# Values and sums of the exponentials of a windowed attention in four column tiles, with the own heads picked by DMA

## The chip, the cores and the metric

The kernel runs on one core of a Trainium2 chip. The metric is the device time of one execution in microseconds. A core has the engines PE (TensorE, matrix products), DVE (VectorE), ACT (ScalarE, activations), POOL (GpSimd) and SP (SyncE, which here only issues DMAs). Each runs its own instruction stream in order, and they meet at semaphores.

## The reference

Two layers over 8 sequences of 512 tokens with 128 channels. Layer 0 adds to x a Mamba block (projection, convolution, a scan with 16 states over time, gate) and a mixture of eight experts. Layer 1 is the part that the change touches:

```python
xn = layernorm(x)
q, k, v = split_heads(xn @ Wq + bq), split_heads(xn @ Wk + bk), split_heads(xn @ Wv + bv)   # 16 heads of 8
probs = softmax(q @ k.T / sqrt(8) + mask)        # mask: |i - j| <= 32
x = x + (probs @ v) @ Wo + bo + (silu(xn @ wg) * (xn @ wu)) @ wd
```

## The kernel before

**The order of the work.** Every engine walks through the same list of units. One turn of the list is an iteration of 28 slots. Three lanes run in it, each for another sequence: `pre` (projections and convolution for the next sequence), `scan` (the scan of layer 0: 16 steps, in slots 0, 1, 3, 5, 7, 8, 10, 12, 14, 15, 17, 19, 21, 22, 24, 26) and `attn` (layer 1 of the sequence before). `finish` is the end of layer 1 of the sequence before that one. The tables PRE_AT, LAYER1_AT, FINISH_AT and EDGE say in which slot a unit stands; EDGE's come first in slot 0, and within a slot the order is exp, values, scores, step, averages, sum, rowmax, turn, then finish, attn and pre. Eight sequences give seven iterations with both a scan and attention, one with attention alone, and a last one with only the finish.

**A step of the scan** is on VectorE the scan (L705, 128x1024) and the product dBu (L697), on ScalarE two exponentials dA (L901), on GpSimd the product hc (L1066), and on TensorE the sum into y_bank (L1151). At the end of the scan y_bank is gated (L800), and TensorE multiplies with out_proj (L1196).

**Attention.** 512 queries are 16 groups g of 32. The 128 partitions hold 4 heads x 32 queries, and r = 0 to 3 counts four such sets (a head is 8 of the 32 channels of a set r). For each group: `scores` (L1224, L1226) writes 128 x 4 x 96 into a PSUM bank, `rowmax` (DVE L820), `exp` (ACT L983, four instructions), `turn` (four transposes L1232 to PSUM, and ACT's copy pT, L988). Every second group there is a unit of `values` (L1240): with pT as the stationary operand it gives 128 partitions (head, query) x 33 columns, the 32 channels of all four heads of a set and, since vw has a column of ones, the sum of the exponentials; the 33 columns are computed three times (VREP) and read once. `averages` on VectorE takes the reciprocal of the sums (L831) and multiplies, in four instructions, each head's own 8 channels by it (L835). In slot 0 of the next iteration `attnT` transposes the averages (L1252, L1254), ACT adds the bias bv (L994); in slot 3 `fin` (L1261, L1266, L1270) adds the feed-forward part and the product with Wo, and in slot 4 `y_out` (DVE L848) adds x1.

**Banks.** Layer 1 has three PSUM banks, called work, work_l and more in the profile (0, 1, 2 in L1_BANK), which its units take in a fixed turn: `fin` uses 0, as do out, q, v1, the even scores and turns; the values and the gates of the feed-forward part use 2.

**Tables of ScalarE.** Functions come in table sets. The loads stand where the function changes: ahead of the logarithm (L944, slot 24) and ahead of the next exponential.

**SP's queue** issues the rows of B and C for each step of the scan (L526, three steps ahead), x_in, x_res and the output. The chip's time before the first attention iteration (some 245 us) goes to the experts and the first scan.

## Time and profile before

| | |
|---|---|
| median of 3 runs | 1190.73 us (1190.7 to 1194.21) |
| profiled execution, its own time | 1193.12 us |
| its span, first to last instruction | 1191.1 us |
| mean granted TensorE clock | 0.923 of full speed |
| busy: PE, DVE, ACT, POOL | 78%, 71%, 51%, 35% of the span |

The rows in the section on the trace come from this one profiled execution. Busy shares are means over the whole span. In a row, "x16" is the number of instructions merged into it; "[0.76 <-ACT pT L988]" says how long the engine had been idle and which instruction released it. A float32 matrix product is two instructions in the trace (two passes), a transpose one. A term of a sum is compared with the profiled execution's 1193.12 us, and a forecast with the median.

### The profile page before, as it was taken

The numbers are of one execution on the slowest core, as the hardware profiler recorded it, in microseconds if no ns is written. First come the engines' busy times: TensorE is split into PE (matmuls) and PEld (weight loads), VectorE is DVE, ScalarE is ACT, GpSimd is POOL, SyncE is SP. The second block draws the span as 40 slices with busy tenths as digits, with TensorE's granted clock in tenths as the row PEclk, the third lists the DMA queues.
The fourth block names the chain that finished last, engine by engine and source line by source line (L and its number), as shares of the span: only waits on it lengthen the run. The fifth ranks groups of instructions, "written<-read, shape, count | busy, mean of one in ns | idle before, by whom it ended". The sixth has DMA issues, their size and how long they took to land.

```text
span 1191.1 us, 13478 instructions
## 1 busy us (share of the span) xinstructions
PE 923.4 (78%) x4474; PEld 585.3 (49%) x4474; DVE 849.0 (71%) x1301; ACT 613.0 (51%) x1410; POOL 411.1 (35%) x234
## 2 busy tenths in 40 slices
PE   3553888857887788778887788878787878788786
PEld 2412676734554455545454455545554545445555
DVE  7772543669779877888688868886978788767232
ACT  2142555635655655564566455655645564654542
POOL 2274222233622362237213722363226423532000
PEclk9566999987999899999999899989998999999998
DMA  8163878843322332233223321333233223430000
GB/s 277 40 216 125 235 234 294 239 110 86 81 65 75 90 82 73 66 79 89 73 70 90 89 73 54 90 92 87 54 80 87 76 66 83 99 80 1 10 1 9
DMA packets 79540, 116.65 MB, mean 98 GB/s; under 512 B 4848, under 2 KB 40048, under 8 KB 79344
## 3 DMA queue, kind: packets, MB, share of 16 engines
q1 hardware_dynamic: 73184, 108.99, 33.5%
q0 software_dynamic: 6288, 6.82, 2.5%
q8 instruction: 35, 0.57, 0.2%
q14 instruction: 33, 0.27, 0.1%
HBM read 103.73 MB, written 12.06 MB: 97 GB/s over the span
## 4 chain that ended last, share of the span: by engine, by line
PE 37%; DVE 19%; issue 17%; POOL 13%; ACT 10%; DMA 3%; SPq 0%; POOLq 0%; DVEq 0%; ACTq 0%
PE y_bank L1151 11%; DVE hst L705 7%; POOL hc L1066 7%; PE more L1240 7%; POOL xs_d L1034 3%; POOL x_res L1050 3%; ACT pexp L983 3%; PE work_l L1232 3%; DVE dBu L697 2%; ACT pT L988 2%; PE work_l L1226 2%; PE work L1232 2%; PE work L1170 2%; DMA hst<-in_hidden 1%; PE more L1248 1%
## 5 line engine op out<-in xcount | busy, mean ns | idle before, releaser
L1066 POOL TENSOR_TENSOR hc<-hst,bcr 128x1024 f32<-128x1024 f32 x116 | 280.2, 2415 | 607.8 <-DVE dBu L697 607.8
L1151 PE MATMUL y_bank<-hc,pk 128*128 128x512 f32 x512 | 275.0, 664 | 68.6 <-POOL hc L1066 59.7
L705 DVE TENSOR_TENSOR_SCAN hst<-dA,dBu 128x1024 f32<-128x1024 f32 x128 | 291.6, 2278 | 5.7 <-ACT dA L901 4.9
L1151 PEld LDWEIGHTS y_bank<-hc,pk 128*128 128x128 f32 x512 | 100.6, 208 | 183.9 <-POOL hc L1066 83.9
L901 ACT ACTIVATE dA<-dt,neg_a 128x511 f32<-128x511 f32 x256 | 171.4, 726 | 17.3 <-DVE hst L705 15.8
L697 DVE TENSOR_TENSOR dBu<-dtu,bcr 128x1024 f32<-128x1024 f32 x128 | 157.9, 1234 | 12.7
L1240 PE MATMUL more<-vw,pT 96*128 96x99 f32 x1024 | 131.0, 280 | 37.3 <-ACT pT L988 25.9
L1240 PEld LDWEIGHTS more<-vw,pT 96*128 96x128 f32 x1024 | 121.2, 194 | 69.3 <-issue 38.1
L988 ACT COPY pT<-work 96x512 f32<-96x512 f32 x64 | 37.2, 581 | 157.4 <-PE work L1232 157.4
L820 DVE TENSOR_REDUCE nmax<-work 128x4 f32<-128x384 f32 x64 | 35.4, 554 | 62.6 <-PE work L1226 62.6
L988 ACT COPY pT<-work_l 96x512 f32<-96x512 f32 x64 | 37.2, 581 | 63.9 <-PE work_l L1232 63.9
L983 ACT ACTIVATE pexp<-work,nmax 128x96 f32<-128x96 f32 x256 | 65.8, 343 | 6.3 <-DVE nmax L820 6.1
L983 ACT ACTIVATE pexp<-work_l,nmax 128x96 f32<-128x96 f32 x256 | 65.9, 341 | 5.7 <-DVE nmax L820 5.5
L835 DVE TENSOR_TENSOR attn<-more,rden 32x64 f32<-32x64 f32 x256 | 55.9, 218 | 8.1
L1050 POOL DMA_INDIRECT x_res<-ys_d,slot_b x32 | 51.8, 1620 | 9.3 <-issue 9.3
L1232 PEld LDWEIGHTS work_l<-pk,pexp 128*96 128x96 f32 x256 | 28.0, 127 | 51.0 <-ACT pexp L983 31.2
L1226 PE MATMUL work_l<-kT,qbd 128*128 128x384 f32 x128 | 52.3, 490 | 0.0
L1226 PE MATMUL work<-kT,qbd 128*128 128x384 f32 x128 | 51.8, 487 | 0.0
L1232 PEld LDWEIGHTS work<-pk,pexp 128*96 128x96 f32 x256 | 29.9, 127 | 41.2 <-issue 20.7
L1164 PE MATMUL work<-xnT,pk 128*128 128x512 f32 x64 | 38.4, 686 | 14.2 <-ACT hs L914 9.4
L1232 PE MATMUL work_l<-pk,pexp 128*96 128x128 f32 x256 | 39.7, 277 | 12.4 <-ACT pexp L983 12.1
L1232 PE MATMUL work<-pk,pexp 128*96 128x128 f32 x256 | 40.2, 281 | 11.8 <-ACT pexp L983 11.8
(296 smaller groups left out, 1422.0 us busy)
## 6 DMA issues: line engine op xcount, KB each, us to landing
bcr<-bc_d SPq DMA_DIRECT2D x128, 512.0 KB, 4.9
qbd<-in_wx SPq DMA_DIRECT2D x8, 578.0 KB, 3.9
attn<-in_wx SPq DMA_DIRECT2D x8, 578.0 KB, 4.3
pT<-in_wx SPq DMA_DIRECT2D x8, 578.0 KB, 5.7
kT<-in_wx SPq DMA_DIRECT2D x8, 578.0 KB, 5.3
vw<-in_wx SPq DMA_DIRECT2D x8, 578.0 KB, 5.0
xs_d<-rbuf POOLq DMA_DIRECT2D x1, 2560.0 KB, 9.7
hst<-in_hidden SPq DMA_DIRECT2D x8, 256.0 KB, 5.8
```

The lines of the kernel that those rows point to most:

```text
L697: v.tensor_tensor(dBu[:], dtu[par], bcr[n % RING][:, 0:1, :].to_broadcast([P, NH, L]), ALU.mult).then_inc(s_dBu, 1)
L705: v.tensor_tensor_scan(hst[n % 2][:].rearrange("p h t -> p (h t)"), dA[n % 2][:].rearrange("p h t -> p (h t)"), dBu[:].rearrange("p h t -> ...
L835: last = v.tensor_tensor(attn[:, k - 1:k + 1, :, j, :], o[q, :, :, HD * j:HD * j + HD], rden[q, :, :].unsqueeze(3).to_broadcast([32, 2, RG ...
L901: s.activation(dA[n % 2][:, h, 1:L], dt[par][:, h, 1:L], ACT.Exp, scale=neg_a[:, h, n:n + 1]).then_inc(s_dA, 1)
L983: last = s.activation(pexp[k % 2][:, r, :], w1k(f"s{k}")[:, r * KW:(r + 1) * KW], ACT.Exp, bias=nmax[:, k, r:r + 1])
L988: s.copy(pT[k % 4][:], w1k(f"pT{k}")[0:KW, :]).then_inc(free1(f"pT{k}"), 1)
L1050: g_.indirect_dma_start(x_res[:, j, :], None, ys_d.rearrange("i j p d -> (i j p) d"), bass.IndirectOffsetOnAxis(ap=slot_b[:, j:j + 1], axi ...
L1066: g_.tensor_tensor(hc[n % 2][:], hst[n % 2][:], bcr[n % RING][:, 1:2, :].to_broadcast([P, NH, L]), ALU.mult).then_inc(s_hc, 1)
L1151: last = t.matmul(y_bank[h][:], ident, hc[n % 2][:, h, :], start=False, stop=(n == N - 1))
L1226: t.matmul(w1k(key)[:, 0:RG * KW], qbd[:, k, :, :].rearrange("p h q -> p (h q)"), kT[:, :, k * GQ:k * GQ + KW], start=False, stop=True).th ...
L1232: last = t.transpose(w1k(key)[0:KW, r * P:(r + 1) * P], pexp[k % 2][:, r, :], ident)
L1240: last = t.matmul(w1k(key)[:, a:a + VREP * 33].rearrange("p (n d) -> p n d", n=VREP), pT[(k - 1 + c) % 4][:, r * P:(r + 1) * P], vw[:, k - ...
```

## The change

What was the averages on VectorE becomes a chain over four engines. The roles in `values` are swapped: vw is now stationary (96 x 32 channels of a set r), pT is moving (128 columns: 4 heads x 32 queries), and the result of set r goes to the partitions 32r to 32r + 31. A second matmul with 32 columns of ones as the stationary operand gives the sums of the exponentials on the same partitions. ScalarE copies both to o_all in SBUF. Of the four heads in the columns each partition needs its own, so SP issues 16 DMAs for each half of a sequence, one for each block of 8 partitions, from o_all to o_own. VectorE takes one reciprocal for each half, GpSimd multiplies the whole sequence, ScalarE adds bv. TensorE's transposes fall away. The finish moves: own1 in slot 0, rec1 and avg in slot 5, attnT in slot 6, fin in slot 7, y_out in slot 8. After the last tanh of the feed-forward part the table set with both logarithm and exponential is loaded.

```diff
-VREP = 3
+OWN = 16 * 16
-LAYER1_AT = {0: ["out"], 1: ["x1"], 2: ["ln_a"], 3: ["ln_b"], 4: ["q", "k"], 5: ["v0", "v1"], 6: ["v2", "v3"]}
-FINISH_AT = {2: ["attnT"], 3: ["fin"], 4: ["y_out"]}
-EDGE = [("attn", "y_end"), ("finish", "attnT"), ("pre", "xnT"), ("attn", "gated"), ("attn", "out")]
+LAYER1_AT = {0: ["out"], 1: ["x1"], 2: ["ln_a"], 3: ["ln_b"], 4: ["q", "k"], 5: ["v0", "v1"], 6: ["v2", "v3"], 19: ["own0"], 21: ["rec0"]}
+FINISH_AT = {0: ["own1"], 5: ["rec1", "avg"], 6: ["attnT"], 7: ["fin"], 8: ["y_out"]}
+EDGE = [("attn", "y_end"), ("finish", "own1"), ("pre", "xnT"), ("attn", "gated"), ("attn", "out")]
...
-        vw_all = sb("vw", [P, G, RG, HD * 4 + 1])
+        vw_all = sb("vw", [P, G, RG, HD * 4])
-        attn_all = sb("attn", [P, G, RG, 4, HD])
+        o_all = sb("o_all", [P, 4, 2, G // 2, GQ])
+        ones_v = sb("ones_v", [P, 32])
+        o_own = rbuf[:]
...  SP
+                    if name in ("own0", "own1"):
+                        k = int(name[3:])
+                        q = slice(k * L // 2, (k + 1) * L // 2)
+                        done1(sp, b, f"o{4 * k + 3}")
+                        before(sp, s_avg, b)
+                        for r in range(RG):
+                            for h in range(4):
+                                own = slice(32 * r + HD * h, 32 * r + HD * h + HD)
+                                sp.dma_start(o_own[own, :, q], o_all[own, h, :, :, :].rearrange(
+                                    "p c g q -> p c (g q)")).then_inc(s_own, 16)
...  VectorE
-                    v.memset(vw, 1.0).then_inc(s_clear, 1)
+                    v.memset(ones_v[:], 1.0).then_inc(s_clear, 1)
+                elif name in ("rec0", "rec1"):
+                    k = int(name[3:])
+                    q = slice(k * L // 2, (k + 1) * L // 2)
+                    dve.wait_ge(s_own, (2 * b + k + 1) * OWN)
+                    v.reciprocal(o_own[:, 1, q], o_own[:, 1, q]).then_inc(s_rden, 1)
-                elif name == "averages":
-                    ...
-                    v.reciprocal(rden[:], o[:, :, :, 32]).then_inc(s_rden, 1)
-                    dve.wait_ge(s_rden, b * (G // 2) + k // 2 + 1)
-                    for j in range(4):
-                        last = v.tensor_tensor(attn[:, k - 1:k + 1, :, j, :], ...)
...  ScalarE
                 elif name == "ffn":
                     s.activation(fth[:], w1k(f"gate{k}")[:], ACT.Tanh).then_inc(s_fth, 1)
+                    if k == HC - 1:
+                        s.preload_act_table_set("natural_log_exp_and_others")
+                elif name == "averages":
+                    key = f"o{k // 2}"
+                    full1(act, b, key)
+                    if k in (1, 9):
+                        before(act, s_own, (2 * b + k // 8) * OWN)
+                    g = (k - 1) % 8
+                    for j in range(2):
+                        last = s.copy(o_all[:, :, j, g:g + 2, :].rearrange("p h g q -> p g h q"),
+                                      w1k(key)[:, 2 * P * j:2 * P * j + 2 * P].rearrange("p (g h q) -> p g h q", g=2, h=4))
+                    last.then_inc(free1(key), 1)
                 elif name == "attnT":
-                    full1(act, b, name)
-                    s.activation(attnT[:], w1k(name)[:], ACT.Identity, bias=pc("bv")).then_inc(free1(name), 1)
+                    act.wait_ge(s_avg, b + 1)
+                    done1(act, b, f"up{HC - 1}")
+                    s.activation(attnT[:], fth[:], ACT.Identity, bias=pc("bv")).then_inc(s_attnT, 1)
...  GpSimd
+                    elif name == "avg":
+                        pool.wait_ge(s_rden, 2 * b + 2)
+                        done1(pool, b, f"gate{HC - 1}")
+                        g_.tensor_tensor(fth[:], o_own[:, 0, :], o_own[:, 1, :], ALU.mult).then_inc(s_avg, 1)
...  TensorE
                         for r in range(RG):
-                            a = (c * RG + r) * 33
-                            last = t.matmul(w1k(key)[:, a:a + VREP * 33].rearrange("p (n d) -> p n d", n=VREP),
-                                            pT[(k - 1 + c) % 4][:, r * P:(r + 1) * P],
-                                            vw[:, k - 1 + c, r, :].unsqueeze(1).to_broadcast([KW, VREP, 33]),
-                                            start=True, stop=True)
+                            t.matmul(w1k(key)[32 * r:32 * r + 32, c * P:(c + 1) * P], vw[:, k - 1 + c, r, :],
+                                     pT[(k - 1 + c) % 4][:, r * P:(r + 1) * P], start=True, stop=True)
+                        for r in range(RG):
+                            last = t.matmul(w1k(key)[32 * r:32 * r + 32, (2 + c) * P:(3 + c) * P], ones_v[0:KW, :],
+                                            pT[(k - 1 + c) % 4][:, r * P:(r + 1) * P], start=True, stop=True)
-                elif name == "attnT":
-                    ...
-                    for g in range(G):
-                        last = t.transpose(w1k(name)[:, g * GQ:(g + 1) * GQ],
-                                           attn[:, g, :, :, :].rearrange("p r h d -> p (r h d)"), ident[0:GQ, 0:GQ])
```

## Rows read from the trace of the kernel before

**Rows 1.** The page's part 1: busy us, share of the span, instructions
```profile
PE 923.4 (78%) x4474; PEld 585.3 (49%) x4474; DVE 849.0 (71%) x1301; ACT 613.0 (51%) x1410; POOL 411.1 (35%) x234
```

**Rows 2.** Busy us of each engine in slots 5-9, 15-20 and 21-27
```profile
643.50:664.20 20.70, 14.53 (x65) 8.89 (x64) 20.28 (x16) 12.63 (x21) 7.48 (x3) 0.84 0.39 94
682.50:711.90 29.40, 25.82 (x119) 14.83 (x119) 19.16 (x31) 16.55 (x45) 8.70 (x4) 1.00 0.30 80
711.90:743.90 32.00, 26.45 (x135) 17.01 (x136) 28.57 (x41) 18.15 (x39) 7.04 (x3) 0.95 0.17 50
```

**Rows 3.** Line L800: ns min/median/max, first and last start
```profile
L800 DVE TENSOR_TENSOR dtu<-y_bank,sg x16: 680/686/692, 244.7 to 1100.4; 128x512 f32<-128x512 f32 x16
```

**Rows 4.** The chain that ended last: start, us, what
```profile
605.51 0.45 PE work_l L1232 x4
...
616.59 2.01 PE more L1240 x16
```

**Rows 5.** Groups of instructions: out<-in xcount | busy us, mean ns | idle
```profile
L1066 POOL TENSOR_TENSOR hc<-hst,bcr 128x1024 f32<-128x1024 f32 x116 | 280.2, 2415 | 607.8 <-DVE dBu L697 607.8
...
L835 DVE TENSOR_TENSOR attn<-more,rden 32x64 f32<-32x64 f32 x256 | 55.9, 218 | 8.1
...
L988 ACT COPY pT<-work 96x512 f32<-96x512 f32 x64 | 37.2, 581 | 157.4 <-PE work L1232 157.4
...
L831 DVE RECIPROCAL rden<-more 128x8 f32<-128x8 f32 x64 | 13.1, 204 | 47.8 <-PE more L1240 47.4
...
L884 ACT ACTIVATE pT<-work 128x128 f32<-128x128 f32 x14 | 3.9, 276 | 25.5 <-PE work L1122 25.5
...
L755 DVE TENSOR_REDUCE ss<-xsq 128x4 f32<-128x256 f32 x8 | 3.3, 412 | 1.4 <-ACT xsq L928 1.4
...
L679 DVE MEMSET vw<- 96x2112 f32 x1 | 1.8, 1818 | 0.4 <-issue 0.4
```

**Rows 6.** Timeline of slots 21-27: start, us, engine, line [idle <-releaser]
```profile
716.92 0.58 ACT L988 COPY pT<-work 96x512 f32<-96x512 f32 x1 [3.66 <-PE work L1232]
...
726.56 1.88 PE L1151 MATMUL y_bank<-hc,pk 128*128 128x512 f32 x4
...
729.52 1.28 ACT L944 ACT_TABLE_LOAD   x1
...
734.27 0.95 PE L1232 MATMUL work<-pk,pexp 128*96 128x128 f32 x4 [1.82 <-ACT pexp L983]
...
735.02 3.30 PE L1151 MATMUL y_bank<-hc,pk 128*128 128x512 f32 x4
...
739.51 2.00 PE L1240 MATMUL more<-vw,pT 96*128 96x99 f32 x16 [0.76 <-ACT pT L988]
...
742.79 1.23 DVE L697 TENSOR_TENSOR dBu<-dtu,bcr 128x1024 f32<-128x1024 f32 x1
```

**Rows 7.** The timeline of slots 3 and 4
```profile
641.04 0.69 DVE L848 TENSOR_TENSOR y_out<-x1r,work 128x512 f32<-128x512 f32 x1 [5.39 <-PE work L1270]
...
642.27 0.60 ACT L919 ACTIVATE tg<-work 128x512 f32<-128x512 f32 x1 [0.28 <-PE work L1164]
```

**Rows 8.** The timeline of slots 8 and 9
```profile
658.54 3.78 PE L1151 MATMUL y_bank<-hc,pk 128*128 128x512 f32 x4 [5.02 <-POOL hc L1066]
...
662.11 2.24 PE L1170 MATMUL work<-pk,u 128*128 128x96 f32 x16
```

**Rows 9.** The timeline of the iteration with attention alone
```profile
1119.70 0.53 PE L1224 MATMUL work<-bandb,identb 128*128 128x384 bf16 x1
```

**Rows 10.** SP's queue: a DMA issue of 64 KB
```profile
688.66 0.32 SPq L533 DMA_DIRECT2D bc_d<-dtT  x1
```

**Rows 11.** DMA issues: out<-in xcount, KB each, median us to landing
```profile
bcr<-bc_d SPq DMA_DIRECT2D x128, 512.0 KB, 4.9
...
bc_d<-dtT SPq DMA_DIRECT2D x8, 64.0 KB, 1.7
```

**Rows 12.** The timeline of the tail; the span ends at 1191.1
```profile
1187.67 0.69 DVE L848 TENSOR_TENSOR y_out<-x1r,work 128x512 f32<-128x512 f32 x1 [7.34 <-PE work L1270]
```

32 lines of the change are left out of this document (9 added, 23 removed).

## The prediction, made before the changed kernel had run

> **What bounds the kernel now.** The page comes first, for the balance of the engines: TensorE is busy for 78% of the span and VectorE for 71% [rows 1], so neither average decides; they are both full somewhere, and the question is where. The table of stretches splits one steady iteration (L800, which opens one, runs in pairs from 244.7 to 1100.4 us, so seven iterations with a scan take 122.2 us each; one with attention alone follows, and a tail) [rows 2, 3]. What the reader should see: in slots 5 to 9 (643.5 to 664.2) VectorE is busy 20.3 of 20.7 us; in slots 15 to 20 (682.5 to 711.9) TensorE is busy 25.8 of 29.4; in slots 21 to 27 both are nearly full, VectorE 28.6 and TensorE 26.5 of 32.0. So the same microsecond is worth something different in each stretch, and I make the sum by stretch.
>
> **The values and their row sums.** Now a unit is 8 matmuls with the 96x128 pT stationary and 99 columns moving; the trace has two passes for each, and the chain shows 16 passes in 2.01 us, 0.125 each [rows 4]. After: 16 matmuls, 32 passes, 32 stationary columns and 128 moving ones. The trace has a pass with 128 moving columns and 96 stationary ones, the transposes of L1232: four in 0.45 us, 0.112 each [rows 4]. Their smaller stationary operand did not hold them back, so I take 0.112 as the time for which a pass streams. One after another, 32 passes would be 3.6 us, 1.6 more than now. No two matmuls of this trace write different groups of 32 partitions, so whether column tiles run side by side is not shown. Bounds: 3.6 us, and a quarter of it, 0.9, if four always ran together. I take a value between: the two passes of one matmul need the same tile and can't overlap, and they are issued back to back; so if matmuls begin in order, the second pass of one tile can run only beside the first pass of the next. That makes 17 streams of 0.112, 1.9 us, a gain of 0.1. The nearest rows speak for order: in every group of matmuls the passes stand in the order in which they were issued.
>
> The Trainium skill (TensorE: Matmul & The Clock Gate, section Part 3: Packing small matmuls) says that column tiles run concurrently and that matmuls start and end strictly in order; it gives 2.38x for three column tiles with 512 columns. By that speedup alone a unit would be 3.6 / 2.38 = 1.5 us (an estimate); by its rule of order it is my 1.9. The page on TensorEngine Tiling (Array Packing), section Key Properties, adds that a change of the mode drains the array, which this kernel would pay twice in a unit. No run here shows any of the three yet.
>
> **What leaves VectorE, and what comes.** Each unit loses one reciprocal of 0.20 us and four products of 0.22: 1.1 us in 64 units [rows 5]. ScalarE gets two copies of 256 columns: between the 0.28 us of 128 columns and the 0.58 us of 512 lies 0.38, so 0.75 us a unit [rows 5]. They stand ahead of the copy of pT in ScalarE's queue, and that copy waits for TensorE, 3.66 us before 716.92 [rows 6], so they are hidden; without that cover they would cost 0.75 x 64 = 48 us. Two reciprocals of 128x256 per sequence are new. The trace has only 128x8 at 204 ns. The products of 64 columns take 218 ns and a reduction of 256 takes 412, 1.0 ns a column and 153 to start; so the 8 columns cost 51 ns, some 6 ns each [rows 5]. Bounds for 256 columns: 0.42 us if those 51 ns are a fixed cost, 1.7 us at 6 ns a column. I take 1.7, as the one row of this operation has it. (The Trainium skill, VectorE: DVE Perf Modes, section First, the fixed hardware budget, says that a reciprocal runs with a repeat count of 8. At its 0.96 GHz that would be 2.1 us and the start, an estimate on the same side.)
>
> **Slots 21 to 27.** VectorE loses three units there (3.5 us and a wait of 1.2) and gains the first reciprocal, 1.7. The table load of 1.28 us ahead of the logarithm goes, and the second one behind it, ahead of the exponentials [rows 6]: with them TensorE waited 1.82 us for the exponentials and then ran four passes of L1151 in 3.30 us, which take 1.88 at the full clock. The load moves behind the last tanh in slot 20, ahead of the same wait of 3.66 us [rows 6]. I follow the two queues from 711.9. The first reciprocal makes step 13 begin 0.7 us late; the missing averages give this back by step 14; the transposes of group 14 start at 732.5 instead of 734.3; values 15 start at 736.8 instead of 739.5 [rows 6]. VectorE is then the later one: steps 15, hc, dtu and dBu end at 741.3 instead of 744.0, because 1.2 of averages and 1.0 of waiting drop out in front of dBu. The gated product follows at once: **-2.7 us** an iteration. The transposes of attnT on TensorE in slot 0 lie in the shadow of the gated product: nothing.
>
> **Slots 0 to 9.** Here lies the largest wait that the change removes: VectorE stands 5.39 us before y_out, because fin is in front of it, and conv1 is queued behind [rows 7]. But what is late next? sg0, behind conv1, wants tanh of zg0 (642.27 [rows 7]), and that follows ScalarE's normalised rows and a TensorE transpose, not fin. It gains about 1.6 us, and pays 1.28 for the table load that now stands before this tanh: -0.4. From there VectorE is full to slot 9, and gets the second reciprocal (+1.7) and y_out (+0.7). Sum: **+2.0**. Fin (32 passes and the one of the bias, some 4 us on TensorE by the pass of [rows 4]) fills the hole of 5.02 us before 658.54, which also spares the passes behind it the low clock (3.78 us instead of 1.88 [rows 6, 8]). X_dbl, now at 662.11, could then follow u, which VectorE has ready at 660.8; y_out makes u 0.7 late, and the rest of that wait goes: **-0.6**. GpSimd's product is half of the 2.42 us of 128x1024, 1.2 us, and lies in the 608 us in which it waits for VectorE [rows 5].
>
> **Slots 10 to 20.** TensorE is the bound (VectorE is busy 19.2 of 29.4 us [rows 2]); averages that stand ahead of a row maximum cost only where the exponentials wait for it, for which I give half of one unit's 1.1: -0.5. Five units give 5 x 0.1: **-1.0** together.
>
> An iteration is -2.7 + 2.0 - 0.6 - 1.0 = -2.3, seven of them -16.1.
>
> **The ends.** In the iteration with attention alone TensorE has no hole in slot 7: the first scores start at 1119.70 right behind v3 [rows 9]. Fin (4.0 at the full clock, 0.5 more for a cold start) and y_out (0.7) now lie between, since both use one bank: +5.2; the units give 0.8 back: **+4.4**. At the very end the chain is now: values end 1179.1, two copies 0.75, sixteen DMA issues, the landing, reciprocal 1.7, product 1.2, attnT 0.69, eight passes of wo at half the clock 8 x 2 x 0.112 = 1.8, y_out 0.69, and 2.7 from there to the end [rows 12]. The issue of 64 KB takes 0.32 us of SP, and they land in 1.7 us [rows 10, 11]: 16 x 0.34 = 5.4 and 1.7. That ends at 1195.9 instead of 1191.1: **+4.8**. The memset of vw, 1.82 us, becomes one of 32 columns [rows 5]: **-1.7**.
>
> Sum: -16.1 + 4.4 + 4.8 - 1.7 = -8.6 us against the profiled execution's 1193.1, which stands 2.4 above the median of 1190.7 (its span is 1191.1, so 2.0 lie around it). On the scale of the median: 1182.
>
> **SP's queue.** In slots 15 to 20 three units take 29.4 us [rows 2], 9.8 each. The sixteen issues in slot 19 begin with the copies of unit 7, take 5.4 us and land 1.7 later, 7.1 in all; ScalarE's copy of unit 9, which waits for them, is ready 9.8 after that of unit 7: 2.7 us of slack. The rows of B and C for step 14 are issued behind them and land 4.9 us later [rows 11], 10.7 after the copies of unit 7; the product that wants them follows step 13 in slot 22, some 16 after them. In slot 0 the rows of step 3 stand behind the issues in the same way, and have two steps and a slot without a step to spare; x_in stands there too, which nobody wants before the next iteration.
>
> **The rivals.**
> 1. *Tiles exclude each other* (slower). A unit takes 3.6 us, 1.7 above my value. It costs 43 units in full (five of each full iteration, all eight of the last), 73 us, and the other 21 some 21 after VectorE's slack: 1182 + 94 = 1276. For it: the trace shows no overlap of any two passes. Against: separate groups of columns. It decides from 2.1 us a unit on.
> 2. *All four tiles overlap.* A unit of 0.9 to 1.4 us, since 32 weight loads have a price that no row shows alone: 43 x 0.5 to 1.0 = 22 to 43 us less, some 1150. Against it stand the two passes of each matmul. (The page's 1.5 us for a unit would give 1182 - 43 x 0.4 = 1165, an estimate.)
> 3. *The reciprocal costs as little as another operation*, 0.42 us: 1.3 x 15 = 19 us less, 1163.
> 4. *The picks come late.* At 0.6 us an issue the sixteen take 9.6 and 1.7, and unit 9 waits 1.5 us, and the rows of B and C behind them as much: 10 to 25 us more, 1192 to 1207. It decides from 0.5 us an issue on.
>
> **Chances.** Forecast 0.40 (its own range 1170 to 1197), serial tiles 0.18, four-fold overlap 0.15, cheap reciprocal 0.13, late picks 0.14. The predicted time is 1182. A range from 1140 to 1235 leaves out the serial tiles and little else. Within 0.3% (3.6 us, about what this kernel's measurements tell from nothing) lies a quarter of the forecast and a little of the fourth rival: 0.13. Faster: 0.52, of which 0.24 from the forecast and 0.28 from the second and third rivals. Slower: 0.35.
>
> **What would show it.** The unit's length on TensorE in the iteration without a scan (1.9; 3.6 or 1.2 for the rivals); the mean of the new reciprocal (1.7); no wait of ScalarE before the unit 9 copies for a DMA; one table load in slot 20 and one before the tanh of zg0; no 5.4 us wait before y_out, but VectorE full from slot 4 on; scores 5 us later after v3 in the last iteration; a tail 5 us longer. The prediction is wrong if a unit is not near 1.9 us, since each 0.1 us there is 4 us of time, or if TensorE's clock, which is at its lower level behind the hole before 658.54 [rows 8], falls in slots 3 and 4 too, where fin leaves a hole.

## The result: 1197.99 us, slower by 0.4%

| | median us (runs) | ratio to before, 95% interval |
|---|---|---|
| before | 1193.89 (1190.7 to 1196.67, 20 runs) | |
| after | 1197.99 (1193.43 to 1207.09, 20 runs) | 1.0039 (1.0026 to 1.0052) |

The forecast was 1182 and faster. The time lies in the range and on the other side of no change. The twenty executions of after spread over 14 us, and the time goes with the granted clock (0.919 in the shortest, 0.901 in the longest). The profiled execution of after took 1201.56 us, its span is 1199.5, and its mean granted clock 0.915. The page shows less work on TensorE and VectorE [rows 1] and a longer span:

```profile
PE 874.3 (73%) x5362; PEld 510.9 (43%) x5362; DVE 828.6 (69%) x997; ACT 649.5 (54%) x1541; POOL 422.7 (35%) x242
```

The two halves of the span go in opposite directions. The gated product, one for each iteration (L812 in after, L800 before), is the mark: its first pair starts at 242.6 us (244.7 before), its last at 1091.6 (1099.8 before). So the seven iterations between take 849.0 us, 6.1 less than before. The first and the last of the seven are shorter by 4.0 us each; the five between take 615.0 us together, and 613.0 before. But from the last gated product to the end it is 107.9 us, and 91.3 before: 16.6 more. With the 2.1 us of the start that is 8.4, the whole difference of the spans. Forecast were -16.1, +9.2 and -1.7.

### What the trace of after shows

Groups of instructions by line and form (busy us, mean ns of one, idle time before them):

```profile
L709 DVE TENSOR_TENSOR dBu<-dtu,bcr 128x1024 f32<-128x1024 f32 x128 | 167.6, 1309 | 16.0 <-DMA bcr<-bc_d 3.1 <-DVE hst L717 0.5
...
L744 DVE SCALAR_TENSOR_TENSOR z<-hs,half_c,z 128x512 f32<-128x512 f32 x48 | 56.3, 1223 | 0.0
...
L1002 ACT COPY o_all<-more 128x256 f32<-128x256 f32 x128 | 41.7, 385 | 60.2 <-DMA rbuf<-o_all 35.5 <-PE more L1260 24.7
...
L834 DVE RECIPROCAL rbuf<-rbuf 128x256 f32<-128x256 f32 x16 | 28.0, 1750 | 44.5 <-DMA rbuf<-o_all 44.5
...
L795 DVE TENSOR_TENSOR dc<-tg,dc 128x1024 f32<-128x1024 f32 x8 | 14.4, 1794 | 0.5 <-ACT tg L945 0.5
...
L1100 POOL TENSOR_TENSOR fth<-rbuf 128x512 f32<-128x512 f32 x8 | 12.4, 1549 | 91.8 <-DVE rbuf L834 91.8
```

The reciprocal of 256 columns takes 1.75 us (forecast 1.7), the copy 0.385 (0.38). New is the waiting: ScalarE stands 35.5 us in all before its copies for the picks' DMA, and VectorE 44.5 us before the reciprocals. And VectorE's operations on other lines have become slower: L744 1223 ns in place of 1049, L795 1794 in place of 1224, dBu 1309 in place of 1234.

The line of the picks in SP's queue (ns min/median/max, first and last start):

```profile
L554 SPq DMA_DIRECT2D rbuf<-o_all x256: 679/686/1292, 331.7 to 1187.9; - x128
```

The timeline of one iteration (its gated product is at 617.0 us): the passes behind fin in slot 8 (653.38), the collision in slots 12 to 14 (671.76), the picks of slot 19 and who waits for them, the last passes and the next gated product (736.53); then a unit of values without a scan beside it (1124.89), and the tail:

```profile
653.38 3.15 PE L1169 MATMUL y_bank<-hc,pk 128*128 128x512 f32 x4 [2.93 <-POOL hc L1080]
...
671.76 2.93 POOL L1080 TENSOR_TENSOR hc<-hst,bcr 128x1024 f32<-128x1024 f32 x1
...
673.59 3.01 DVE L709 TENSOR_TENSOR dBu<-dtu,bcr 128x1024 f32<-128x1024 f32 x1
674.08 1.43 POOL L1073 TENSOR_TENSOR xdn<-xdr,pk 128x384 f32<-128x384 f32 x1
...
674.74 3.56 PE L1169 MATMUL y_bank<-hc,pk 128*128 128x512 f32 x4 [1.96 <-POOL hc L1080]
...
699.61 11.65 SPq L554 DMA_DIRECT2D rbuf<-o_all  x16
...
712.64 1.75 DVE L834 RECIPROCAL rbuf<-rbuf 128x256 f32<-128x256 f32 x1 [1.99 <-DMA rbuf<-o_all]
712.70 0.65 ACT L1002 COPY o_all<-more 128x256 f32<-128x256 f32 x2 [3.98 <-DMA rbuf<-o_all]
...
713.88 0.50 PE L1242 MATMUL work<-bandb,identb 128*128 128x384 bf16 x1 [3.80 <-ACT pT L989]
...
715.45 3.61 PE L1169 MATMUL y_bank<-hc,pk 128*128 128x512 f32 x4
...
736.53 3.39 PE L1169 MATMUL y_bank<-hc,pk 128*128 128x512 f32 x4 [1.53 <-DVE hc L732]
...
739.96 1.29 DVE L812 TENSOR_TENSOR dtu<-y_bank,sg 128x512 f32<-128x512 f32 x2 [1.08 <-PE y_bank L1169]
...
1124.89 0.43 PE L1257 MATMUL more<-pT,vw 96*32 96x128 f32 x8 [1.50 <-DVE fsg L841]
...
1125.13 0.40 PE L1260 MATMUL more<-pT,ones_v 96*32 96x128 f32 x8
...
1125.35 0.40 PE L1257 MATMUL more<-pT,vw 96*32 96x128 f32 x8
...
1125.57 0.40 PE L1260 MATMUL more<-pT,ones_v 96*32 96x128 f32 x8
...
1125.90 0.34 PE L1242 MATMUL work_l<-bandb,identb 128*128 128x384 bf16 x1
...
1175.99 0.65 ACT L1002 COPY o_all<-more 128x256 f32<-128x256 f32 x2 [1.28 <-PE more L1260]
...
1176.66 11.96 SPq L554 DMA_DIRECT2D rbuf<-o_all  x16
1190.02 1.75 DVE L834 RECIPROCAL rbuf<-rbuf 128x256 f32<-128x256 f32 x1 [18.01 <-DMA rbuf<-o_all]
1191.85 1.26 POOL L1100 TENSOR_TENSOR fth<-rbuf 128x512 f32<-128x512 f32 x1 [85.35 <-DVE rbuf L834]
```

How to read it. The four groups of eight passes start 0.22 us apart, and the next matmul of another kind follows 1.01 us after the first (1124.89 to 1125.90): a unit is 1.0 us, not 1.9, and not 2.01 as before [rows 4]. The sixteen picks in slot 19 hold SP for 11.65 us, 0.73 each, where the prediction had 5.4 in all. ScalarE's copy of unit 9 starts at 712.70, 3.98 us late; pT is queued behind it, so TensorE stands 3.80 us, and the passes behind the hole run at the lower of its two levels, 1.2 GHz in place of 2.4 (L1169: 3.61 us in place of 1.88 [rows 6]; granted clock 0.53 in these 3.6 us). VectorE's first reciprocal waits 1.99 us for the same picks. In the tail the picks hold SP for 11.96 us, and the reciprocal starts 13.4 us after the first issue.

Count also the groups of four passes into y_bank that run wholly or in part at the lower level. Before there are three in an iteration: in slot 1, in slot 8 and in slot 26 [rows 6, 8]. In this iteration of after there are four: behind a hole of 2.93 us in slot 8, behind 1.96 us at 674.74, behind the picks, and behind 1.53 us at 736.53. For the last of them the next gated product waits 1.08 us. So fin has not filled the hole in slot 8, it has shortened it from 5.02 to 2.93 us, and the passes behind it still take 3.15 us.

The starts of the groups' scores (L1242; L1224 before) in us after the gated product, worked out from the timelines of one iteration each:

```
group             0     4     5    11    12    13    next gated product
before          43.1  57.0  63.3  92.6  96.4 102.5   122.9
after           41.7  54.9  63.6  90.0  96.9 104.3   123.0
```

This is the table that says where the gain went. Up to group 4 after is 2.1 us ahead. From 4 to 5 it loses 2.4. From 5 to 11 it gains 2.9, three units of one microsecond each. From 11 to 13 it loses 4.4 to the picks. The rest is 1.7 shorter. Sum: 0.1. The means of the five middle iterations say the same (group 4 at 54.9 for 56.7, group 5 at 63.9 for 63.0, group 11 at 90.6 for 92.3, group 13 at 104.4 for 102.2, the gated product at 123.0 for 122.6).

### The profile page after: what moved, and what is told of

It reads as the page before. It is cut to its first block, busy times and chain, and to the rows that moved or that the text cites. A ratio compares the mean times of both kernels' runs of the same rounds, so it can differ in the third digit from the quotient of the medians.

```text
span 1199.5 us, 15327 instructions
## 1 busy us (share of the span) xinstructions
PE 874.3 (73%) x5362; PEld 510.9 (43%) x5362; DVE 828.6 (69%) x997; ACT 649.5 (54%) x1541; POOL 422.7 (35%) x242
## 4 chain that ended last, share of the span: by engine, by line
PE 29%; DVE 24%; issue 15%; ACT 11%; POOL 10%; SPq 7%; DMA 4%; DVEq 0%; POOLq 0%; ACTq 0%
PE y_bank L1169 9%; DVE hst L717 8%; SPq L554 7%; POOL x_res L1064 4%; POOL hc L1080 3%; POOL xs_d L1048 3%; DVE dBu L709 3%; DVE z L744 2%; ACT pT L989 2%; PE work_l L1250 2%; ACT pexp L984 2%; ACT dA L902 2%; PE work L1244 1%; DMA hst<-in_hidden 1%; PE more L1257 1%
## 5 line engine op out<-in xcount | busy, mean ns | idle before, releaser
L1169 PE MATMUL y_bank<-hc,pk 128*128 128x512 f32 x512 | 279.9, 674 | 74.6 <-POOL hc L1080 57.1
L1169 PEld LDWEIGHTS y_bank<-hc,pk 128*128 128x128 f32 x512 | 102.6, 211 | 189.9 <-issue 91.6
L709 DVE TENSOR_TENSOR dBu<-dtu,bcr 128x1024 f32<-128x1024 f32 x128 | 167.6, 1309 | 16.0 <-DMA bcr<-bc_d 3.1
L1257 PE MATMUL more<-pT,vw 96*32 96x128 f32 x1024 | 54.9, 282 | 39.3 <-ACT pT L989 25.9
L837 DVE TENSOR_REDUCE nmax<-work_l 128x4 f32<-128x384 f32 x64 | 35.5, 554 | 59.0 <-PE work_l L1244 58.9
L1002 ACT COPY o_all<-more 128x256 f32<-128x256 f32 x128 | 41.7, 385 | 60.2 <-DMA rbuf<-o_all 35.5
L1242 PE MATMUL work<-bandb,identb 128*128 128x384 bf16 x64 | 22.3, 348 | 61.2 <-ACT pT L989 60.2
L834 DVE RECIPROCAL rbuf<-rbuf 128x256 f32<-128x256 f32 x16 | 28.0, 1750 | 44.5 <-DMA rbuf<-o_all 44.5
L1257 PEld LDWEIGHTS more<-pT,vw 96*32 96x32 f32 x1024 | 27.7, 110 | 71.7 <-issue 38.4
L744 DVE SCALAR_TENSOR_TENSOR z<-hs,half_c,z 128x512 f32<-128x512 f32 x48 | 56.3, 1223 | 0.0
L1260 PE MATMUL more<-pT,ones_v 96*32 96x128 f32 x1024 | 54.3, 277 | 0.0
```

The costliest lines, as they stand in the source:

```text
L709: v.tensor_tensor(dBu[:], dtu[par], bcr[n % RING][:, 0:1, :].to_broadcast([P, NH, L]), ALU.mult).then_inc(s_dBu, 1)
L744: v.scalar_tensor_tensor(z[k % 2][:, h, :], hs[:, h, tap:tap + L], half_c[:, h * KC + tap:h * KC + tap + 1], z[(k - 1) % 2][:, h, :], ALU. ...
L1169: last = t.matmul(y_bank[h][:], ident, hc[n % 2][:, h, :], start=False, stop=(n == N - 1))
L1257: t.matmul(w1k(key)[32 * r:32 * r + 32, c * P:(c + 1) * P], vw[:, k - 1 + c, r, :], pT[(k - 1 + c) % 4][:, r * P:(r + 1) * P], start=True, ...
```

## The experiments

Each kernel is timed against the kernel before on the same chip; the ratio is to that. Those of the picks, the tiles and the last queue start from after, those whose name begins with "before" or "finish" from before.

### Do column tiles run side by side?

**One tile**, and **pairs on a tile**:

```diff
 one_tile
-  t.matmul(w1k(key)[32 * r:32 * r + 32, c * P:(c + 1) * P], vw[...], pT[...])     # ones alike
+  t.matmul(w1k(key)[0:32, c * P:(c + 1) * P], vw[...], pT[...])
 pairs_on_a_tile
-  for r in range(RG): values(c, r)
-  for r in range(RG): ones(c, r)
+  for r in range(RG): values(c, r); ones(c, r)
```

> The changed kernel with all sixteen matmuls of a values unit writing partitions 0 to 31, that is, one column tile in place of four; the results of three of the four row groups are not written. The order of two and two on one tile cost nothing to speak of (a unit 1.06 us in place of 1.01). Theory 'column tiles run side by side, and the chip looks past the two matmuls ahead of it': with one tile nothing can run side by side, 32 passes of 0.11 us, 3.5 us a unit, and 40 to 60 such units: 1300 to 1350 us. Rival 'a pass with a stationary operand of 32 columns is simply short (0.027 us), whichever tile it is in': a unit stays at 1.0, and the time at 1198 within 5 us.

> The changed kernel with the same sixteen matmuls of a values unit in another order: values and ones of one column tile behind one another, so that four passes in a row want the same tile. In the changed kernel eight passes of four tiles take 0.22 us, as though all four tiles ran side by side. Theory 'tiles run side by side, and matmuls begin in order': 25 streams of 0.11 us are left in a unit, 2.8 us in place of 0.9; with 40 to 60 units that count, 1275 to 1310 us. Rival 'the passes are short for another reason' or 'each tile has its own queue, whatever the order': no change, 1198 within 3 us.

One tile (three quarters of the results are not written): 1294.11 us, 1.0837 (1.0823 to 1.0851). Pairs on a tile: 1203.32, 1.0087 (1.0068 to 1.0107). The values in the iteration with attention alone, first one tile, then pairs (here ones is L1259):

```profile
1221.88 1.03 PE L1257 MATMUL more<-pT,vw 96*32 96x128 f32 x8 [0.76 <-ACT pT L989]
...
1222.75 1.04 PE L1260 MATMUL more<-pT,ones_v 96*32 96x128 f32 x8
...
1223.63 1.04 PE L1257 MATMUL more<-pT,vw 96*32 96x128 f32 x8
...
1224.50 1.04 PE L1260 MATMUL more<-pT,ones_v 96*32 96x128 f32 x8
```

```profile
1128.21 0.45 PE L1257 MATMUL more<-pT,vw 96*32 96x128 f32 x8 [1.50 <-DVE fsg L841]
...
1128.45 0.43 PE L1259 MATMUL more<-pT,ones_v 96*32 96x128 f32 x8
...
1128.67 0.44 PE L1257 MATMUL more<-pT,vw 96*32 96x128 f32 x8
...
1128.89 0.44 PE L1259 MATMUL more<-pT,ones_v 96*32 96x128 f32 x8
...
1129.27 0.34 PE L1242 MATMUL work_l<-bandb,identb 128*128 128x384 bf16 x1
```

In one tile eight passes take 0.875 us, 0.109 each, which is the pass of the prediction; in four tiles 0.22. So the four tiles run fully side by side. A unit is 2.5 us longer in one tile, 160 us in 64 units, of which 96 show in the time. A unit in four tiles takes 1.01 us where its 32 passes, four abreast, make 0.87: the change to column tiles and back costs no more than the rest. Pairs on one tile, four passes in a row for the same tile, take 1.06 us a unit in place of 1.01: the chip isn't held up by the order of issue over that distance, which the prediction's 17 streams suppose. What it does inside isn't shown, only that this order costs 0.05 us a unit.

The Trainium skill (TensorE: Matmul & The Clock Gate, section Part 3: Packing small matmuls) has column tiles running concurrently, and the trace agrees: four tiles give 0.875 / 0.22, about 4.0, where the skill's page has 2.38 for three, with 512 columns. By its words that matmuls start and end strictly in order, and if passes on one tile wait for each other, pairs on a tile should have held up the rest; the runs don't bear out the two together, and which of them fails isn't shown.

### What do the picks cost?

```diff
 two_buffers
-  o_all = sb("o_all", [P, 4, 2, G // 2, GQ])
+  o_all = sb("o_all", [P, 2, 4, 2, G // 2, GQ])          # one for each half
 one_pick
-  for r in range(RG):
-      for h in range(4): sp.dma_start(o_own[own, :, q], o_all[own, h, :, :, :])
+  sp.dma_start(o_own[:, :, q], o_all[:, 0, :, :, :])
 picks_in_one_piece
-  sp.dma_start(o_own[own, :, q], ...)                    # two pieces of 1 KB a partition
+  sp.dma_start(o_own[own, k, :], ...)                    # one of 2 KB
```

> The changed kernel with a second copy of o_all, so that ScalarE's copies of unit 9 need not wait for the picks of the first half; the picks themselves stay. Theory 'late picks': in the changed kernel ScalarE waits 4.0 us for the picks in slot 19 (35.5 us in the eight waits together), TensorE stands 3.8 us behind it and then runs at its lower clock. With the wait gone an iteration gets 4 to 6 us shorter, 8 of them 32 to 48: 1150 to 1166 us. Rival 'VectorE decides behind it': the wait lies in front of slots 21 to 27, where VectorE is the bound, so that it only moves: 1188 to 1198, and VectorE is then busy without a gap in slots 21 to 27.

> The changed kernel with one DMA for each half in place of sixteen: it takes the columns of head 0 of each group for all 128 partitions, so the values of the other heads are not the right ones; bytes and everything else are the same. Theory 'late picks': no wait of ScalarE in slot 19, rows of B and C not behind sixteen issues, and a tail 11 us shorter (0.4 in place of 11.6): 8 x 4 to 6 and 11, 1139 to 1155 us. Rival 'VectorE decides': the tail's 11 and no more, 1187. It also prices the sixteen issues against the second copy: the difference to that run is the tail's 11 and what the rows of B and C wait.

> The changed kernel with the picked rows laid out by half, so that each pick writes 2 KB in one piece for each partition and not two of 1 KB. If the 0.68 us of SP for an issue goes with the number of pieces, it falls to some 0.35 us, sixteen take 5.5 us, and the time falls to 1150 to 1170 (with 'late picks'). If it is the price of any small DMA here, it stays 0.68 us, and the time 1198 within 3 us.

| kernel | us | ratio (95%) |
|---|---|---|
| two_buffers | 1199.3 | 1.0059 (1.0039 to 1.0078) |
| one_pick | 1156.75 | 0.97 (0.9675 to 0.9725) |
| picks_in_one_piece | 1185.71 | 0.9941 (0.9929 to 0.9954) |

One pick in place of sixteen (it brings the values of head 0 to all) gives some 41 us against after; of these 20 lie behind the last gated product (87.4 us to the end, 107.9 in after). The sixteen issues are the cost. But a second buffer, which removes ScalarE's wait entirely, gives nothing: in one iteration group 12 comes at 93.3 and group 13 at 99.4 in place of 96.9 and 104.3, and then VectorE waits for the same picks before the first reciprocal, and group 14 is 5.5 us behind group 13 (2.1 in before):

```profile
711.86 1.75 DVE L834 RECIPROCAL rbuf<-rbuf 128x256 f32<-128x256 f32 x1 [1.98 <-DMA rbuf<-o_all]
```

The issue of a pick (the source line of each kernel, ns min/median/max):

```profile
L551 SPq DMA_DIRECT2D rbuf<-o_all x16: 599/600/666, 334.9 to 1144.7; - x16
```

```profile
L554 SPq DMA_DIRECT2D rbuf<-o_all x256: 624/625/1440, 334.4 to 1178.8; - x128
```

The pick of 128 partitions costs SP 600 ns, the one of 8 partitions in two pieces 686, in one piece 625. Neither partitions nor pieces make it dear. Reading SBUF doesn't either: in after the output (out from y_out, L558) reads it and takes 0.38 us, and bc_d from dtT, the row that the prediction used, takes 0.32 [rows 10]; both write DRAM. A bcr issue (L528) reads DRAM and writes SBUF, 0.36. What the picks have and none of these has is SBUF at both ends; no other DMA of that kind was tried. The 61 ns a pick are 1 us for each sixteen, and the time falls by more than 10 us. The expectation had 0.35 us an issue, or no change; it was neither.

Then both deadlines at once, and each alone:

```diff
 one_late_rec (second buffer, one piece), late_rec_one_buffer (one buffer)
-  19: ["own0"], 21: ["rec0"]
+  19: ["own0"]
-  5: ["rec1", "avg"]
+  5: ["rec", "avg"]                                      # v.reciprocal of 2 x 256 columns
```

> The changed kernel with the second copy of o_all, the picked rows in one piece, and one reciprocal of 512 columns in slot 5 in place of one in slot 21 and one in slot 5. With the second copy alone the time stayed at 1199: ScalarE's wait was gone, but VectorE waited 2.0 us for the same picks ahead of the first reciprocal. Theory 'two deadlines on one set of picks': with both gone, the picks cost nothing in slots 19 to 21, and an iteration is as short as with one pick (118.7 us in place of 122.9): 7 x 3 to 4 us less than 1186 of the picks in one piece, 1158 to 1168. Rival 'slots 4 to 9 are full on VectorE': moving 1.7 us of reciprocal there costs as much as it gives, 1180 to 1190.

> The kernel with one late reciprocal, but with the single o_all of the changed kernel: the fourth corner of a square. Picks in one piece in all: both deadlines 1185.7 (measured), neither 1171.5 (measured); the second copy alone took nothing off the changed kernel. Theory 'either deadline alone holds slots 19 to 21': ScalarE still waits 3.4 us in slot 19, the scores of group 12 stay 3 us late, and most of this reaches the gated product: 1180 to 1186. Rival 'only VectorE's deadline counts, because slots 21 to 27 are VectorE's': 1171 to 1174.

| in one piece | reciprocal in slot 21 and 5 | one in slot 5 |
|---|---|---|
| one buffer | 1185.71, 0.9941 | 1189.01, 0.9976 (0.9965 to 0.9987) |
| two buffers | not run (in two pieces: 1199.3) | 1171.5, 0.9821 (0.9795 to 0.9847) |

Neither deadline alone gives time, with one piece a pick the moved reciprocal even costs 3; with both gone 14 us come off at once. Where they come off, in the profiled executions (us):

| | first and last of the seven iterations | the five between | behind the last gated product |
|---|---|---|---|
| picks_in_one_piece (both deadlines) | 235.0 | 603.9 | 106.2 |
| late_rec_one_buffer (ScalarE's) | 233.6 | 600.9 | 108.7 |
| one_late_rec (none) | 228.4 | 596.7 | 99.9 |
| one_pick | 228.3 | 594.5 | 87.4 |

Behind the last gated product either deadline alone is enough to hold the work: of the 17 us between the second and the third row 8.8 lie there, and two_buffers, which has VectorE's deadline alone, needs 107.2 there. In the five middle iterations this isn't shown. With the reciprocal moved and one buffer ScalarE still waits 3.0 us, but four of the five take 119.3 to 119.6 us, as long as with both deadlines gone (118.3 to 120.5), and one takes 123.2. The measured 1189 is above what either theory gave for this kernel (1180 to 1186, 1171 to 1174). An experiment that takes away one of two waits for the same event shows nothing, and that isn't evidence against the event.

```diff
 last_on_two_queues: of the second half's sixteen picks in the last two sequences, eight issued by ScalarE
 tail_by_halves: in the last sequence reciprocal and product of the first half before the last picks land
 spread_picks: four picks a slot, in slots 19 to 22 and 0 to 3; each of the three stands on the one before, the first on one_late_rec
-  19: ["own0"]
+  19: ["own00"], 20: ["own01"], 21: ["own02"], 22: ["own03"]
```

> The kernel with one late reciprocal, and the second half's picks of the last two sequences issued by SP and ScalarE, eight each, in place of sixteen by SP. Behind the last values nothing but the picks is left, and behind the sequence before them fin waits in front of the scores. Theory: the tail is 8 x 0.62 = 5 us shorter and the start of the last sequence's scores up to 4 us earlier: 7 to 9 us less than the kernel with one late reciprocal. Rival 'the two queues share what makes an issue slow': 1.2 us for an issue, and no change.

> The kernel with the last picks on two queues, and in the last sequence the reciprocal and GpSimd's product taken for each half by itself, so that the first half's are out of the way before the last picks land. The tail loses 1.7 us of reciprocal and 0.6 of product: 2.3 us less than the kernel with the last picks on two queues, 1163 to 1167. A rival only in size: GpSimd's second product beside nothing, so that no more than the reciprocal's 1.7 comes off.

> The kernel with the tail by halves, and the sixteen picks of a half in four slots, four each, in place of one run of ten us in SP's queue. In the kernel with one late reciprocal VectorE waits 16.4 us in all for rows of B and C that are issued behind the picks (3.1 us in the changed kernel, where other waits covered it). Theory: that wait goes, and 8 to 16 us with it: 1150 to 1158. Rival 'the wait lies in slack': nothing, 1163 to 1167.

1167.83, 0.9781 (0.9768 to 0.9793); 1164.97, 0.9778 (0.9765 to 0.979); 1160.81, 0.9734 (0.9713 to 0.9755). Eight issues on each of two queues take 5.6 and 6.0 us side by side, so the queues don't share what makes an issue slow. The first gives some 4 us of the 7 to 9 expected. The step from the first to the second is within the intervals; their traces have 95.7 and 93.6 us behind the last gated product (99.9 in one_late_rec), near the 2.3 expected. In the third VectorE's wait for rows of B and C, 16.6 us in all, is gone, as the theory has it, and 4 us of the 8 to 16 come off.

### The other parts alone, and why they don't add up

```diff
 before_finish
-FINISH_AT = {2: ["attnT"], 3: ["fin"], 4: ["y_out"]}
+FINISH_AT = {6: ["attnT"], 7: ["fin"], 8: ["y_out"]}
 before_table
+                    if k == HC - 1: s.preload_act_table_set("natural_log_exp_and_others")
 before_finish_table: both; finish_table_late_bc and spread_late_bc: bc (xdn) in slot 14, not 13
```

> The kernel before with one part of the change alone: the transposes of attnT in slot 6, fin in slot 7, y_out in slot 8 (before: 2, 3, 4). By the prediction's steps, without table and reciprocal: sg0 1.6 us earlier, y_out 0.7 in the full stretch, 0.6 from the hole, so 1.5 us less in each of seven iterations, and 5.2 more in the iteration with attention alone: 1192 - 10 + 5 = 1187. Rival 'VectorE loses it to GpSimd': the convolution's products, which now start 5 us earlier, lie beside GpSimd's product of 128x1024 and get slower (3.51 us for two in place of 1.4 in the changed kernel): 1193 to 1200.

> The kernel before with one part of the change alone: the table of the logarithm and the exponential loaded behind the last tanh, in slot 20. The prediction has 1.28 us for the load ahead of the logarithm and as much for the second behind it, both in front of the exponentials for which TensorE waited 1.82 us and ran 1.4 us at its lower clock. If that is worth what the prediction gave: 1.0 to 2.5 us in each of eight iterations, 8 to 20 us, 1171 to 1183. Rival 'ScalarE is ahead of VectorE there': no change, 1190 to 1193.

> The kernel before with the finish in slots 6 to 8 and the table loaded in slot 20, the values as they were. Alone the two gave 13.0 and 4.3 us. If they add up: 1174. Then the values in tiles with well-placed picks (1160.8) are worth 13 us, most of it in the iteration with attention alone. Rival 'TensorE has no slack in slots 21 to 27, so the table needs the shorter units': 1177 to 1180. Rival 'the values in tiles are worth nothing': 1158 to 1163.

> The kernel before with finish, table and GpSimd's product xdn in slot 14. If the side by side of dBu and GpSimd costs here as well (the scores of group 5 start 7.6 us after those of group 4 with the finish moved, 6.3 in the kernel before): 1 to 2 us an iteration, 1160 to 1167. If it is only the slot that changes: 1172 to 1176.

| kernel | us | ratio (95%) |
|---|---|---|
| before_finish | 1178.4 | 0.9894 (0.9878 to 0.9909) |
| before_table | 1189.38 | 0.9963 (0.995 to 0.9976) |
| before_finish_table | 1189.66 | 0.9987 (0.9973 to 1.0001) |
| finish_table_late_bc | 1189.67 | 0.9986 (0.9966 to 1.0006) |

The moved finish is by itself worth 13 us, twice its forecast, and it loses nearly all of it when the table moves too. Putting xdn one slot later in that kernel changes nothing (1189.67). The traces say part of why the gain is lost. The timelines of three kernels, at the passes into y_bank that follow a hole (slot 1 and slot 8 of before; the same two of before_finish; slot 14 of two iterations of before_finish_table):

```profile
751.35 3.65 PE L1151 MATMUL y_bank<-hc,pk 128*128 128x512 f32 x4 [2.12 <-POOL hc L1066]
...
781.47 3.78 PE L1151 MATMUL y_bank<-hc,pk 128*128 128x512 f32 x4 [5.02 <-POOL hc L1066]
```

```profile
743.14 1.98 PE L1151 MATMUL y_bank<-hc,pk 128*128 128x512 f32 x4 [2.12 <-POOL hc L1066]
...
769.99 1.98 PE L1151 MATMUL y_bank<-hc,pk 128*128 128x512 f32 x4 [1.15 <-POOL hc L1066]
```

```profile
796.72 1.99 PE L1153 MATMUL y_bank<-hc,pk 128*128 128x512 f32 x4 [1.62 <-POOL hc L1068]
...
916.87 3.43 PE L1153 MATMUL y_bank<-hc,pk 128*128 128x512 f32 x4 [1.63 <-POOL hc L1068]
```

Read the number in brackets and then the duration. The same 2.12 us of idle time is followed by 3.65 us for four passes in before and by 1.98 in before_finish, where the hole of 5.02 us in slot 8, which fin now fills, has become 1.15. That the one brings the other isn't shown: in before itself the hole of 2.12 us is once followed by four passes in 1.98 us (at 384.12, in the second iteration). In the steady iteration of before_finish the granted clock is 1.00 throughout, in before it is 0.94, with three slow groups an iteration; the iteration takes 119.1 us for 122.9. And in before_finish_table a hole of 1.62 us leaves the clock alone in one iteration, and one of 1.63 in the next brings 3.43 us: iterations of 120.1 and 121.9 us take turns. So the time here depends on whether the clock falls behind a hole, and this on more than the hole's length. It isn't all: without a slow group this iteration still takes 120.1 us for 119.1, and of the 11.8 us between the two spans 3.9 lie behind the last gated product. For these no cause was looked for.

The last two runs put work into the holes and move nothing:

```diff
 before_filled {0: 10, 4: 26}, spread_filled {0: 10, 4: 20, 7: 10, 14: 6}
+                for _ in range({0: 10, 4: 26}.get(n, 0)):
+                    t.matmul(y_bank[0][:, 0:RG * KW], nil[:], bandb[:, 1, :, :].rearrange("p r k -> p (r k)"),
+                             start=False, stop=False)
                 pe.wait_ge(s_hc, b * N + n + 1)
```

> The kernel before, unchanged but for 10 and 26 such matmuls in front of the sums of steps 0 and 4 (holes of 2.1 and 5.0 us). If the clock alone makes the 3.8 us that the finish gives in an iteration (119.1 in place of 122.9), filling the holes gives as much without moving anything: 2 x 1.7 us an iteration, 1192 - 8 x 2 to 3.5: 1164 to 1176. If the gain of the moved finish was VectorE's wait before y_out, which stays here: 1190 to 1195.

> The kernel with spread picks, and in front of the sums of steps 0, 4, 7 and 14 (where TensorE stands 2.1, 3.8, 2.3 and up to 1.5 us) 10, 20, 10 and 6 matmuls of 128x384 bf16 with a stationary operand of zeros, which add nothing to y_bank; the queue runs them before the wait. Theory 'the clock is what the shorter units give back': the passes behind the holes, 3.4 to 3.8 us in slots 1, 8 or 26, take 1.98, two such groups an iteration are gone, 3.2 us, of which half to all shows: 1135 to 1150. Rival 'the fill is in the way, or zeros do not keep the clock': 1158 to 1175.

1181.62, 0.9906 (0.9881 to 0.9931), and 1157.82, 0.9707 (0.9695 to 0.972), 35 us under the kernel before; only one_pick, which picks one head for all, is as fast. before_filled at the places of before's 751.35 and 781.47:

```profile
746.42 1.79 PE L1152 MATMUL y_bank<-bandb,nil 128*128 128x384 bf16 x10
...
748.04 1.88 PE L1156 MATMUL y_bank<-hc,pk 128*128 128x512 f32 x4
...
771.18 4.39 PE L1152 MATMUL y_bank<-bandb,nil 128*128 128x384 bf16 x26
...
776.37 1.98 PE L1156 MATMUL y_bank<-hc,pk 128*128 128x512 f32 x4 [0.80 <-POOL hc L1068]
```

Matmuls that add zeros stand where TensorE stood idle (L1152), and the four passes behind them take 1.88 and 1.98 us. Nothing else has changed but the passes' own time, so the gain of 11 us is the clock's; the mean granted clock of the execution is 0.962 in place of 0.923, and 1.00 in a steady iteration. It is less than the 16 to 28 us expected. A steady iteration takes 120.1 us, 2.8 less than before, and before_finish has 3.8 less: the clock is worth most of what the moved finish gives, and the rest may be the wait before y_out or what the fill itself costs. In the spread kernel the same fill takes nearly all slow groups away too (0.955 for 0.930), and gives only 3 us where 11 to 26 were expected; what holds the iteration there instead was not tried.

### What is left of the units' gain?

> The kernel with spread picks, with a reciprocal of 8 columns in place of 512 in all sequences but the last, so that the averages of these are not divided rightly. Theory 'slots 4 to 9 are VectorE's': 3.1 us of 3.35 go, and nearly all of it shows: 7 x 3.1 = 22 us, 1139 to 1145. Rival 'it lies under the exchange of TensorE and ScalarE': 1155 to 1161.

> The kernel with spread picks, and GpSimd's product xdn in slot 14 in place of 13. In the kernel with one late reciprocal that product and the one of hc lie beside VectorE's dBu of step 7, which takes 3.15 us where it takes 1.23 alone, and the scores of group 5 start 7.4 us after those of group 4 (6.3 in the kernel before). Theory 'side by side they slow each other': dBu falls to 1.3 to 2.2, and 1 to 2 us an iteration come off: 1146 to 1154. Rival 'dtT is late then, or the next product is beside it': 1159 to 1164.

The first is slower than the spread kernel, by some 4 us and just clear of the intervals, and the second gives nothing: 1164.39, 0.9774 (0.9758 to 0.9789), and 1161.14, 0.9741 (0.9726 to 0.9756). With 3.1 us of VectorE's work gone from slot 5, the scores of group 0 start at 42.1 us in the mean of the five middle iterations, in the spread kernel at 43.3. But then it takes 9.1 us from group 4 to group 5, in the spread kernel 7.5, and the iteration is 119.4 us long for 118.7. Between these groups one finds this:

```profile
784.33 2.27 DVE L719 TENSOR_TENSOR_SCAN hst<-dA,dBu 128x1024 f32<-128x1024 f32 x1
...
785.38 2.94 POOL L1090 TENSOR_TENSOR hc<-hst,bcr 128x1024 f32<-128x1024 f32 x1
...
786.71 3.54 DVE L711 TENSOR_TENSOR dBu<-dtu,bcr 128x1024 f32<-128x1024 f32 x1
787.70 1.45 POOL L1083 TENSOR_TENSOR xdn<-xdr,pk 128x384 f32<-128x384 f32 x1
...
788.38 3.12 PE L1187 MATMUL y_bank<-hc,pk 128*128 128x512 f32 x4 [2.48 <-POOL hc L1090]
```

GpSimd's product hc starts beside VectorE's scan, and dBu, which takes 1.23 us alone, takes 3.54 beside hc and xdn. TensorE waits 2.48 us for hc and runs four passes in 3.12. Moving xdn one slot back takes it away from this dBu (1.35 us in two of the five iterations, 2.2 to 2.4 beside hc in the others; 2.2 to 3.3 in the spread kernel), but it then lies beside the next one (1.59), and the scores start where they did. That dBu takes longer beside GpSimd is measured; how much of the iteration this sets is not settled by these runs, nor is what made the kernel with the short reciprocal slower.

The Trainium skill (GPSIMD Engine Reference, section Specifications) says that GpSimd shares its SBUF interfaces with VectorE and contends with instructions that have two SBUF inputs. The trace agrees: dBu has two (dtu, bcr) and goes from 1.23 to 3.54 us. The scan beside the same hc (row L719 at 784.33 in that kernel, 2.27 us) has its dBu in PSUM and takes what all scans of that kernel take, 2.27 to 2.29 us.

## Why the prediction was wrong, by its own steps

**The unit of values** was mis-stepped, in the favourable direction: "the second pass of one tile can run only beside the first pass of the next" gives 1.9 us; it is 1.0. The pass of 0.112 was right (0.109 in one tile), and so was the slow bound (3.6; 3.5 measured with one tile). The second rival's mechanism is the true one, at its fast end. Its gain of a microsecond a unit is there wherever TensorE has the say: 2.9 us in groups 5 to 11 (the prediction had 1.0 for slots 10 to 20).

**SP's queue** is the step that turned the sign. The term of 0.34 us an issue was taken from a DMA with SBUF at one end and DRAM at the other [rows 10]; a pick, SBUF at both ends, takes 0.69 and sixteen of them 11.65, more than the 0.5 from which the fourth rival decides and above its example of 0.6. The slack of 2.7 us was counted for ScalarE's unit 9 and the rows of B and C, and not for the first reciprocal in slot 21, which waits for the same picks (1.98 to 2.52 us an iteration; ScalarE 3.97 to 4.52). Both mechanisms that the prediction set at 0.15 and 0.14 are true at once, and almost cancel, which its separate rivals did not allow for: one pick gives the 1157 that belongs to the second rival, sixteen cost 41 us on top.

**Copies, reciprocal, product.** Right: 0.385 for 0.38, 1.75 for 1.7; the product is 1.26 in the tail for 1.2 and 1.55 in the mean. The third rival is false. The copies are hidden as forecast (one_pick has ScalarE waiting 23.4 us before them, for TensorE alone).

**Slots 21 to 27**: -2.7 forecast, +1.9 measured, from the values in slot 20 to the next gated product (34.0 us, 705.93 to 739.96; before 32.2, 711.89 to 744.05). The path was wrong as well as the picks: VectorE was to be the last before the gated product, but it waits 1.08 us there for TensorE, whose last four passes run in 3.39 us. So the slow group of 3.30 us [rows 6] isn't spared, it has moved behind another hole, and that without late picks too: one_pick has it in four of its five middle iterations (3.17 to 3.68 us). The spread kernel needs 17.5 to 19.0 us from group 13 to the gated product and before 20.4, but without the reciprocal of 1.75 there.

**Slots 0 to 9**: +1.4 forecast with fin's 0.6, measured -1.4 at the scores of group 0. The wait of 5.4 us before y_out went, as said. That fin fills the hole before 658.54 [rows 8] and spares the passes behind it the low clock did not come true in after (2.93 us and 3.15 us at 653.38); it did in before_finish, where no group of the steady iteration is slow and group 0 comes at 38.9 in place of 43.1. After has in these slots, besides the finish, the reciprocal, the table load and slower products beside GpSimd (the first two of L744 take 3.51 us at 631.38), and is 2.8 us later than before_finish; no run parts the three. That VectorE's work gets dearer beside GpSimd was in none of the sums.

**The table**: alone 4.3 us of gain (0.9963), about half a microsecond an iteration, where 8 to 20 us in all were expected.

**The ends.** Attention alone: the scores start 24.4 us after the gated product for 19.9, +4.5, where fin and y_out were to cost +5.2. The tail from the last copies: 11.6 us longer for 4.8; the issues are 6.6 of the difference of 6.8. The gain of the units in the last sequence, 5.4 and 6.9 us a pair of groups for 6.4 and 7.9, is lost to one wait of 6.4 for the first half's picks. The memset is 0.09 us for 1.82, as forecast. The 2.1 us by which the first gated product comes earlier can't be put down to it: in the other kernels with this memset it comes at 242.1 to 246.4 us.

## What to carry to other kernels

Price a DMA by a row of the same kind, source and target memory included, and count every deadline of what it brings: a wait with two takers moves when only one is relieved. Ask of each hole in TensorE's row what its clock does behind it, before asking what fits into the hole. Column tiles are worth using for products with 32 output channels: four of them gave four times the rate here, in both orders of issue that were tried, but the gain shows only where the values' results can be taken away in time.

## What the runs showed of the hardware

- Four column tiles of 32 stationary columns and 128 moving ones, float32: 8 passes in 0.22 us; the same in one tile 0.875.
- An SBUF to SBUF DMA holds SP's queue for 0.60 to 0.69 us, whether it moves 16 KB in 8 partitions or 256 KB in 128; one from DRAM to SBUF (L528) 0.36, from SBUF to DRAM 0.32 to 0.38 (L533 of before, L558). Two queues issue side by side at 0.69 to 0.83 us each.
- The granted clock falls or doesn't behind holes of the same length (2.12 us: 3.65 or 1.98 us for four passes; 1.62 and 1.63 us: 1.99 and 3.43), and with matmuls of a zero operand in the holes it stays up (1.00 in a steady iteration of before_filled, 0.94 in before).
- VectorE's product dBu of 128x1024 takes 1.23 us alone and up to 3.54 us beside GpSimd's products. The reciprocal takes 1.75 us for 256 columns and 3.35 for 512.
